# New weights by kind of step in the planner that fixes the order of every engine's queue

## The reference

```
x = _L0_xattn_ref(x, ctx_1024, ...)
x = _L1_xattn_ref(x, ctx_1024, ...)
x = _L2_xattn_ref(x, ctx_1024, mask_1xS2_bf0, ...)
x = _L3_xattn_ref(x, ctx_1024, ctx_1024, mask_BxSxS2_ik1, ...)
```

## Time and profile before

| | us |
|---|---|
| median of 3 runs (4792.21 to 4800.22) | 4799.45 |
| the profiled execution | 4795.66 |
| its span, first to last instruction | 4793.9 |
| TensorE busy | 4336.8 |
| VectorE busy | 2966.2 |
| ScalarE busy | 2755.4 |
| GpSimd busy | 1568.3 |

### The profile page before, as it was taken

The page is one execution under the profiler, slowest core; times in us unless marked ns, Lnnn a source line. Parts: engine busy times, 40 slices in busy tenths (PEclk is TensorE's granted clock), DMA queues, the critical chain, the costliest instruction groups (busy, mean ns, idle before and its releaser), DMA issues.

```text
span 4793.9 us, 87224 instructions
## 1 busy us (share of the span) xinstructions
PE 4336.8 (90%) x32576; PEld 2984.8 (62%) x32576; DVE 2966.2 (62%) x6391; ACT 2755.4 (57%) x4392; POOL 1568.3 (33%) x1172
## 2 busy tenths in 40 slices
PE   7998989989899898998989899898998989989886
PEld 4565656666566665666656566665766656666554
DVE  7746567575765747667475675757657476574634
ACT  3554656656556575655656556565665655557443
POOL 4422233332323323233232333323233242332212
PEclk9999999999999999999999999999999999999997
DMA  2000000000000000000000000000000000000000
GB/s 87 1 1 1 1 9 1 10 1 1 9 1 10 1 1 9 2 9 1 9 1 1 9 1 9 1 1 9 1 10 1 1 9 1 9 1 3 1 3 3
DMA packets 34187, 29.67 MB, mean 6 GB/s; under 512 B 9768, under 2 KB 33264, under 8 KB 33520
## 3 DMA queue, kind: packets, MB, share of 16 engines
q1 hardware_dynamic: 33776, 24.08, 1.7%
HBM read 19.88 MB, written 4.19 MB: 5 GB/s over the span
## 4 chain that ended last, share of the span: by engine, by line
PE 68%; DVE 19%; ACT 6%; issue 4%; POOL 1%; DMA 1%; SPq 1%; DVEq 0%; ACTq 0%; POOLq 0%
PE ps L907 14%; PE ps L920 10%; PE ps L994 9%; PE ps L987 8%; PE ps L931 6%; DVE mx L1286 4%; DVE pr L1292 4%; PE ps L881 3%; PE ps L940 3%; DVE kx L1382 2%; PE ps L910 2%; PE ps L890 2%; PE ps L865 2%; PE ps L952 1%; DVE st L1209 1%
## 5 line engine op out<-in xcount | busy, mean ns | idle before, releaser
L1470 POOL TENSOR_TENSOR kx<-kT,k_sb 128x616 f32<-128x616 f32 (+1 forms) x704 | 1039.0, 1476 | 1724.7 <-PE ps L907 794.8
L907 PE MATMUL ps<-kx,qT 128*128 128x308 f32 (+1 forms) x2816 | 1085.3, 494 | 34.5 <-DVE pr L1292 18.7
L1286 DVE TENSOR_REDUCE mx<-ps 128x8 f32<-128x616 f32 (+1 forms) x704 | 671.5, 954 | 669.7 <-PE ps L910 406.1
L1105 ACT ACTIVATE pr<-pr 128x616 f32<-128x616 f32 (+1 forms) x704 | 586.0, 839 | 664.2 <-DVE pr L1292 659.3
L1114 ACT ACTIVATE pt<-ps 77x512 f32<-77x512 f32 (+1 forms) x1408 | 777.4, 589 | 304.1 <-PE ps L920 302.1
L920 PE MATMUL ps<-k_sb,pr 128*77 128x128 f32 (+1 forms) x5632 | 811.6, 280 | 93.0 <-ACT og L1123 30.6
L920 PEld LDWEIGHTS ps<-k_sb,pr 128*77 128x77 f32 (+1 forms) x5632 | 636.2, 146 | 328.7 <-issue 165.6
L1292 DVE TENSOR_TENSOR pr<-ps,mx 128x616 f32<-128x616 f32 (+1 forms) x704 | 671.4, 954 | 24.2
L907 PEld LDWEIGHTS ps<-kx,qT 128*128 128x128 f32 x2816 | 485.5, 193 | 288.0 <-issue 214.3
L987 PE MATMUL ps<-hT,w_sb 128*128 128x512 f32 x1024 | 538.3, 632 | 41.9 <-ACT og L1123 35.5
L931 PE MATMUL ps<-pt,v 77*32 77x128 f32 (+1 forms) x11264 | 444.4, 280 | 21.3 <-DVE kx L1382 17.8
(11 more groups left out here) (156 smaller groups left out, 5490.0 us busy)
## 6 DMA issues: line engine op xcount, KB each, us to landing
w_sb<-weights SPq DMA_DIRECT2D x1, 5638.0 KB, 19.9
x<-x SPq DMA_DIRECT2D x16, 256.0 KB
out<-xh SPq DMA_DIRECT2D x16, 256.0 KB, 2.5
cx<-ctx_rows SPq DMA_DIRECT2D x16, 154.0 KB
cT<-ctx_cols SPq DMA_DIRECT2D x16, 154.0 KB
qT<-mask_pairs SPq DMA_DIRECT2D x16, 154.0 KB
w_sb<-weights SPq DMA_DIRECT2D x1, 1280.0 KB
r_sb<-rows SPq DMA_DIRECT2D x1, 522.0 KB
```

The source lines that it names most:

```text
L907: i = mm(o, qT[s][:, b * L:(b + 1) * L], k[:, 4 * j * keys:4 * (j + 1) * keys], start=True, stop=mask is None)
L1105: go_act(v, v, ACT.Exp, scale=t.scale).then_inc(probs_ready.sem, 1)
L1286: link(v_.tensor_reduce(m, tile, AX.X, ALU.max, negate=True))
L1470: tell(pool, g_.tensor_tensor(dst, kT[s][:, b * keys:(b + 1) * keys].unsqueeze(1).broadcast_to([128, 8, keys]), masks.unsqueeze(2).broadca ...
```

## The change

LEAD goes from 3.0 to 4.16461 and STAY from 1.0 to 1.65508. The phases of the streams are written out (0, 0.333333, 0.666667; before 0, 0.333, 0.666). A new table, EAGER, has a number of microseconds for 21 kinds of steps, and it is taken off the key of every part of such a step, on every engine: a positive number puts the kind ahead of the other streams' candidates, a negative one holds it back. Kinds without an entry (`norm`, `rope`, `scores`, `turn`, `mix`, `regroup`, `turn_out`, `gates`, `up`, `down`, `step_size`, `pairs`, `weigh`, `scan`, `turn_gate`, `mamba_out`, `store`) have 0. The earliest start `t` itself isn't changed by it.

```diff
-        done, spent = [], n * PHASE
+        done, spent = [], PHASES[n]
...
-        key = t + LEAD * work[n][m] + (STAY if switch else 0.0)
+        key = t + LEAD * work[n][m] - EAGER.get(step[0], 0.0) + (STAY if switch else 0.0)
...
-LEAD = 3.0
-PHASE = 0.333
-STAY = 1.0
+LEAD = 4.16461
+PHASES = (0, 0.333333, 0.666667)
+STAY = 1.65508
+EAGER = {"load": -1.7, "stats": -0.8, "values": 0.1, "bias": -9.2, "spread": -0.9, "out": 18.4,
+         "bias_mlp": 10.6, "hidden": 0.3, "mlp": 19.7, "project": -0.1, "route": 2.3, "expert_bias": -19.8,
+         "step_size2": 20.2, "conv": 1.5, "decay_in": 0.4, "decay": 20.5, "z": 4.6, "rows": -1.2,
+         "gate_stats": -0.2, "gate_norm": 0.5, "final": -22.1}
```

## The result

| | before | after |
|---|---|---|
| median, us | 4795.83 (4788.0 to 4800.22, 4 runs) | 4600.86 (4600.41 to 4602.18, 4 runs) |
| span of the profiled execution | 4793.9 | 4600.4 |
| TensorE busy | 4336.8 | 4264.4 |
| TensorE idle (span less busy) | 457.1 | 336.0 |
| mean granted TensorE clock | 0.961 | 0.984 |

The changed kernel takes 0.9599 of the time before (95% interval 0.9583 to 0.9614), 195 us less. I had said faster, but 60 us, and the result lies under my range. Of the 193.5 us of the span, 121.1 went out of TensorE's idle time and 72.4 out of its busy time, although it runs the same 32576 instructions.

What follows compares the result with a forecast made beforehand. The prediction took TensorE, busy 90% of 4793.9 us, as the bound. Its terms, -43 - 12 - 15 + 25 - 15 = -60 us, gave 4736 from the profiled 4795.66, or 4740 as the runs' median; range 4665 to 4825.

Steps and rivals of the forecast that it cites:

- The direction and the bound: Whole kernel: faster; only TensorE's 457.1 us idle, ScalarE's table loads in a chain and clock-stretched matmuls can be won.
- The clock: TensorE matmuls slowed by the low clock after stalls in 15 stretches: -12 us, bounds 0 and -30.
- The waits behind `conv`: TensorE's waits behind the Mamba block's `conv` on VectorE (L1382), 86.2 us: half goes, -43, bounds nothing and all.
- STAY and ScalarE: ScalarE: a tenth of 375 table loads go, with some waits on L1123: -15 us, bounds +15 and -40.
- The reserved places: TensorE held for `out`, `mlp` or `decay` whose input isn't there yet: +25 us, floor 0, ceiling about 85.
- the rival's mechanism for slower: Rival 3, TensorE stands reserved: `out` and `decay` at the 85 us ceiling, `conv` gains 20: 4864 us, chance 0.15.
- The thin idle time: Thin TensorE gaps, 233 us, filled by holding back `final`, `expert_bias` and `bias`: -15 us, bounds +30 and -50.
- within a few us, 0: Twelve small entries, mostly on GpSimd or VectorE, such as `load`, `stats`, `project`: 0 us, bounds 10 both ways.
- rival 1: Larger gain: `conv` waits go almost wholly (-80, clock -25), reserved places cost nothing: 4664 us, chance 0.13.

Runs made afterwards that it cites:

- no_project: The changed kernel without the entry of -0.1 us for `project`: 4782.09 us, ratio 0.9975 to the kernel before.
- before_no_tables: The kernel before, order untouched, with gelu, tanh-gelu and silu made plain copies with scale and bias, so no table loads but the first: 4735.89 us, ratio 0.9878.
- no_out: The changed kernel without the entry of +18.4 for `out`: 4735.38 us, ratio 0.9873 to the kernel before.
- searched_old_lengths: The changed kernel with the planner's written lengths kept and all numbers of the key searched anew, TensorE's stalls and clock weighed: 4602.12 us, ratio 0.9591.

## Why the prediction was wrong

*The direction and the bound* were right: TensorE's idle time, its stretched matmuls and ScalarE's loads are what could be won, and all three were. Two terms of the sum were far too small, the clock and the waits on ScalarE, and both came out beyond my bounds.

*The clock* is the term most out of size. I took 12 us and at the most 30, from 15 stretches with 2 us each. TensorE's busy time fell by 72.4. Taken as 2 x (1 - clock) x span, it spent 374 us at 1.2 GHz before and 147 after. The clock records of the two traces agree (372 and 150) and have 61 falls before and 21 after, of which 10 and 9 are in the last 320 us. For 275 us of that time matmuls were running before, for 116 after; half of the difference, 80 us, is my estimate of what the clock gave back, beside the 72.4 measured. I had looked at one kind of stall, and the other waits had falls as well. The group of the `up` matmuls shows it, before and after:

```profile
L987 PE MATMUL ps<-hT,w_sb 128*128 128x512 f32 x1024 | 538.3, 632 | 41.9 <-ACT og L1123 35.5 <-ACT pr L1153 4.0 <-ACT kx L1153 0.7
```

```profile
L991 PE MATMUL ps<-hT,w_sb 128*128 128x512 f32 x1024 | 493.1, 598 | 4.3 <-ACT pr L1157 1.8 <-ACT og L1127 0.8 <-DVE xh L1306 0.7
```

The same 1024 records take 45 us less. Before, 71 of them ran wholly or in part at the low clock, for 0.99 us on average where the others took 0.61; that is 27 us of it. In the changed kernel none did.

*The waits behind `conv`*: -43 predicted, and in the list L1382's 86.2 us became 29.2, so -57. But the reason was wrong. The list names what ended a wait; it doesn't say that a shorter one would have ended it sooner. In that stretch GpSimd's power, the context's norm and the conv hold the same place, and cutting one uncovers the next. I had also said that the same parts of three passes must meet, and VectorE's load in those stretches would keep the stall. The meeting stayed, VectorE's load there rose to 87%, and the stall went. What changed is the order within the meeting: the norm of the context now stands behind the four convs and not between them. VectorE's timeline of the changed kernel, the last conv and then the norm:

```profile
3195.01 2.30 DVE L1386 SCALAR_TENSOR_TENSOR kx<-ps,c_sb,kx 128x508 f32<-128x508 f32 x3
...
3199.86 0.34 DVE L1253 TENSOR_SCALAR xh<-cx,mv,rstd 77x128 f32<-77x128 f32 x1
```

That this place is the reason is argued, and it can't be the only one: in no_project the norm stands behind the second of the four convs, as in the four passes with 4.1 us, and its longest wait behind a conv is 2.1 us.

*STAY and ScalarE*: -15 predicted, -40 the bound. 69 loads fewer where I had said 38; the waits behind `mix`'s copy (L1123) that I quoted, 66.1 us, are 22.3 us at `turn` and 0.8 at `up`. With the other lines they went from 94 to 33 us, which alone is more than the bound. Table loads are not what made these waits: in before_no_tables they are still 91 us. The removal runs put the loads at 41 us of the gain.

The Trainium skill (ScalarE: Activation LUTs, What ACT_TABLE_LOAD costs) puts a drain of about 1380 ns beside each load. The trace has none: in the kernel before, 374 loads follow another operation, and for 321 of them ScalarE's idle time ahead of the load and behind it is under 0.05 us together.

*The reserved places*: +25 predicted, and idle time before L952 and L1034 went from 36.8 to 67.8, which is +31 and inside the 50 to 70 us that I had named. For `out` this was the rival's mechanism for slower, and it was real, at its small end: 22 of the 31 us. For `decay` it wasn't seen. Behind GpSimd's product, the wait that I had priced, L1034 idles 2.7 us before and 3.3 after; the rest stood behind `conv`'s VectorE operations already in the earlier trace rows, 18.8 of 21.5 us, and does so now, 26.7 of 30.0. no_out shows that such a local price doesn't decide: taking it away cost 134 us.

*The thin idle time*: -15 predicted, and not seen. Over the run TensorE idles 121 us less. With all lines counted, the waits behind L1382 went from 88 to 30 us and those behind L1123 from 94 to 33, 119 us together, and the others cancel: +22 at `out`, for one, and -18 behind the gelu of `up` (L1153). Waits of under 1 us grew by 29 us in the middle.

*What failed under all of them* is the sum itself. I treated 21 entries as pushes whose effects add, most of them "within a few us, 0". The planner is a machine that makes one pattern from all numbers together: without the -0.1 us for `project` 181 us are gone, without a digit of the phases 98 us, and LEAD with STAY bring nothing without the table. Such a change can't be priced entry by entry. What could be read beforehand was the size of what a better pattern may win: 24 us of idle time in each pass of 292, and 275 us of matmuls at the low clock, which at the full one would take half. My rival 1 (4664) was the right direction and too small, since it took the clock at 25 us and ScalarE at 15.

What stays open: conv (22 us), table loads (41) and the context's norm (31) add up to 94 of 195 us, each give or take some 20 us, and the first and the third may hold a part in common. Where the gain shows is known: 72 us in busy time, by the clock, and 119 of 121 us of idle time in two groups of waits. Why one order has the waits behind `mix`'s copy and another hasn't was not tested. It is the pattern as a whole, and that is argued from the runs with small edits, not shown by a removal.

## What to carry to other kernels

Where a static order comes from a greedy planner, a weight's size says little about its worth (0.1 us moved this kernel by 181): don't reason on single weights, search, and try the winners on the chip. Truer lengths in the planner may help; one kernel of each, 4562 us against 4602, doesn't settle it. A stall's price on TensorE is its length and half of the time that the matmuls after it run at the low clock; the mean granted clock of the span bounds what a kernel can win back there. Before a releaser named in a list of waits is blamed, look at what stood before it on its own engine. And sort idle time by the length of the waits: here the long ones were the ones that a better order could remove.

## What the hardware showed that I had not expected

- A wait of about 7.6 us costs TensorE 2.4 us of slower matmuls on top, and one of about 2.6 us still 1.4; 16 of the long ones took the mean clock from 0.984 to 0.966.
- VectorE's busy time follows the order, with the same 6391 instructions: 2966.2 us before, 2921.0 after, 3030.3 in searched_old_lengths. The norm of the context (L1249) took 585 ns an operation before and 352 after; GpSimd ran beside 23 of its 64 operations before and beside 3 after. Other operations got slower: the last of `gates` (L1345 after) went from 245 to 1020 ns. Alone it takes 0.19 us; in 13 of 16 passes it now begins 0.06 us into a `spread` of 1.22 us on GpSimd and takes 1.21. The Trainium skill (SBUF — State Buffer, Who interferes with whom) says that the second to come waits for the whole of the other's instruction, and these 13 agree. The planner knows nothing of it. searched_old_lengths has 109 us more of VectorE than the change, with no loss of time; how much of that is GpSimd's doing wasn't counted.
